# Not-left flags from one comparison on VectorE; jump codes scanned four steps after their flags

## The reference, cut to what matters

```
D = pairwise_euclidean(small=layernorm(x), large=ctx)           # 56 x 1500 for each batch
R[i, j] = D[i, j] + min(R[i-1, j], R[i, j-1], R[i-1, j-1])      # cumulative cost
# backtrack from (T1-1, T2-1):
choice = argmin([diag R[i-1, j-1], up R[i-1, j], left R[i, j-1]])
ni = i - 1 if choice <= 1 else i ;  nj = j - 1 if choice in (0, 2) else j
out[j] += rows of the other sequence met on the path
```

## Time and profile before

| what | before |
|---|---|
| median of 3 runs | 534.71 us |
| profiled execution, span from first to last instruction | 538.0 us |
| mean granted TensorE clock | 0.950 of full |
| PE busy | 431.0 us, 80% |
| DVE busy | 376.2 us, 70% |
| ACT busy | 263.5 us, 49% |
| POOL busy | 86.3 us, 16% |

### The profile page before, as it was taken

How to read it: one execution, slowest core, us unless ns; L and a number is a source line. 1 busy time by engine, 2 the same in 40 slices (tenths; PEclk the granted TensorE clock), 3 DMA queues, 4 the chain that set the end, 5 groups by cost and what they waited for, 6 DMA issues and landing times.

```text
span 538.0 us, 10079 instructions
## 1 busy us (share of the span) xinstructions
PE 431.0 (80%) x3977; PEld 249.1 (46%) x3977; DVE 376.2 (70%) x979; ACT 263.5 (49%) x452; POOL 86.3 (16%) x101
## 2 busy tenths in 40 slices
PE   3998877766788878400787899999899899989997
PEld 1344433334556665100233456566566566644444
DVE  7456999999566695885685988889788784271112
ACT  4264888765422393100102456566566567634443
POOL 2000000000100003677891000210210210200000
PEclk9999999989999999755788999999999999999999
DMA  8500266422641202882270003474383382000000
GB/s 287 214 2 0 94 201 186 130 86 86 196 115 57 59 2 66 214 192 85 60 155 18 1 1 76 100 174 94 81 174 78 98 256 60 3 0 1 0 0 17
DMA packets 28718, 50.05 MB, mean 93 GB/s; under 512 B 2464, under 2 KB 18400, under 8 KB 28672
## 3 DMA queue, kind: packets, MB, share of 16 engines
q1 hardware_dynamic: 26848, 45.74, 31.4%
q0 software_dynamic: 1536, 3.67, 2.7%
q10 hardware_dynamic: 288, 0.00, 0.0%
HBM read 39.96 MB, written 9.45 MB: 92 GB/s over the span
## 4 chain that ended last, share of the span: by engine, by line
PE 43%; DVE 37%; issue 8%; POOL 6%; ACT 3%; DMA 2%; DVEq 0%; POOLq 0%
PE banks L1586 7%; PE banks L1562 7%; POOL arena L544 6%; PE banks L1617 5%; DVE arena L1206 5%; DVE mx L1009 4%; DVE work L1235 4%; PE banks L1664 4%; PE banks L1678 4%; DVE arena L1259 2%; PE banks L1292 2%; DVE mx L1017 2%; PE banks L1430 2%; PE banks L1296 2%; DVE work L1201 2%
## 5 line engine op out<-in xcount | busy, mean ns | idle before, releaser
L1009 DVE TENSOR_REDUCE mx<-banks 112x1 f32<-112x500 f32 x168 | 106.9, 675 | 20.2 <-PE banks L1562 20.2
L771 ACT ACTIVATE arena<-banks 128x896 f32<-128x896 f32 x96 | 87.9, 917 | 51.9 <-PE banks L1617 51.2
L1314 PE MATMUL banks<-steps,one 128*128 128x500 f16 (+1 forms) x201 | 56.5, 377 | 32.3 <-DVE hcol L957 32.3
L1586 PE MATMUL banks<-arena 128*32 128x112 f32 (+1 forms) x1536 | 57.3, 265 | 2.9 <-issue 2.0
L1562 PE MATMUL banks<-ctxT,arena 128*112 128x500 bf16 x144 | 54.6, 393 | 5.6 <-issue 1.6
L1586 PEld LDWEIGHTS banks<-arena 128*32 128x32 f32 (+1 forms) x1536 | 33.7, 109 | 24.9 <-issue 20.3
L1235 DVE SCALAR_TENSOR_TENSOR work<-twice,banks,arena 128x202 f32<-128x202 f32 x68 | 29.5, 434 | 19.3 <-PE banks L1430 19.3
L1314 PEld LDWEIGHTS banks<-steps,one 128*128 128x128 f16 x201 | 20.4, 103 | 47.2 <-issue 36.7
L1617 PEld LDWEIGHTS banks<-arena,ctxT 128*128 128x128 bf16 (+1 forms) x576 | 37.3, 104 | 10.5 <-issue 2.8
L1617 PE MATMUL banks<-arena,ctxT 128*128 128x112 bf16 (+1 forms) x576 | 41.1, 213 | 0.6 <-issue 0.6
L544 POOL DMA_INDIRECT arena<-in_w_tab,idx x32 | 33.6, 1051 | 11.6 <-issue 9.4
(11 more groups left out here) (262 smaller groups left out, 751.6 us busy)
## 6 DMA issues: line engine op xcount, KB each, us to landing
ctxT<-key_parts SPq DMA_DIRECT2D x36, 375.0 KB, 6.4
key_parts<-arena SPq DMA_DIRECT2D x32, 281.2 KB, 2.8
ctxT<-in_ctx_T SPq DMA_DIRECT2D x12, 500.0 KB, 8.9
arena<-key_parts SPq DMA_DIRECT2D x12, 375.0 KB, 7.3
ctxT<-in_ctx_nat SPq DMA_DIRECT2D x5, 750.0 KB
arena<-in_ctx_nat SPq DMA_DIRECT2D x3, 750.0 KB
arena<-in_L_ffn_W SPq DMA_DIRECT2D x1, 2048.0 KB, 8.7
arena<-in_fold_w SPq DMA_DIRECT2D x1, 768.0 KB, 5.8
```

Of the source, the lines that this page charges most:

```text
L771: nc.scalar.activation(Pt[0:rows, g % 2, :].rearrange("p (a n) -> p a n", a=2), banks[0:rows, 2 + 2 * (g % 2):4 + 2 * (g % 2), 0:HQ // 2], ...
L1009: nc.vector.tensor_reduce(mx3[:, b % 2, u // NPIECE, u % NPIECE:u % NPIECE + 1], ps[k % 2][0:2 * NJ, 0:PIECE], AX_X, ALU.max).then_inc(s_m ...
L1314: nc.tensor.matmul(bank[:, 0:cols], one16[:, :], steps16[:, 0:cols], start=True, stop=True, skip_group_check=True)
L1586: last = nc.tensor.matmul(ps[6 + b % 2][q:q + 32, o:o + 2 * NJ], vals[0:rows, v0:v0 + 32], Pt[0:rows, g % 2, 2 * t * NJ:2 * (t + 1) * NJ], ...
```

## The change

The flag never is made in one DVE comparison, and ACT's sign instruction, the arrays `rise` and `rises` and two semaphores go. The scan of block k's codes moves from t = 5(k+2)+4 to t = 5(k+2), to where `rows_not_left(k)` was. The lists of the last blocks are reordered.

```diff
             def jump_inputs(k):
                 nc.vector.tensor_tensor(three(left_of(k)), R_slot(t, n, 1, C), R_slot(t, n, 0, C), ALU.is_lt)
-                nc.vector.tensor_tensor(three(rise[k % 2][:, 0:n * C]), R_slot(t + 1, n, 0, C),
-                                        three(mring[...]), ALU.subtract).then_inc(s_rise, 1)
-            def rows_not_left(k):
-                n = CODES[k][1]
-                ve.wait_ge(s_sgn, k + 1)
-                nc.vector.tensor_tensor(never[k % 2][:, 0:n * C], rises_of(k), left_of(k), ALU.is_lt
-                                        ).then_inc(s_nv, 1)
+                nc.vector.tensor_tensor(three(never_of(k)), R_slot(t + 1, n, 0, C),
+                                        three(mring[...]), ALU.is_lt).then_inc(s_nv, 1)
...
                 if t % TB == 0 and t >= 2 * TB:
-                    rows_not_left(t // TB - 2)
+                    jump_targets(t // TB - 2)
                 if t % TB == 1 and t >= TB:
                     jump_inputs(t // TB - 1)
                 if t == STEPS - 2:
-                    rows_not_left(NTB - 2)
                     ve.wait_ge(s_scan, t + 1)
-                    ve.wait_ge(s_code, NTB - 2)
                     jump_inputs(NTB - 1)
-                if t % TB == 4 and t >= 2 * TB:
-                    jump_targets(t // TB - 2)
             ve.wait_ge(s_scan, STEPS)
-            rows_not_left(NTB - 1)
             jump_inputs(NTB)
-            jump_targets(NTB - 2)
-            rows_not_left(NTB)
-            jump_targets(NTB - 1)
-            jump_targets(NTB)
+            for k in range(NTB - 2, NCODES):
+                jump_targets(k)
```

On ACT the function `rise_signs` and its calls go:

```diff
             lane_distances(2)
-            rise_signs(0)
             act.wait_ge(s_w, 16)
             key_step(0)
             lane_distances(3)
             for k in range(2, NTB):
                 for i in KEY_STEPS[k]:
                     key_step(i)
-                    if i == KEY_STEPS[k][0]:
-                        rise_signs(k - 1)
                 if k + 2 < NTB:
                     lane_distances(k + 2)
```

On PE, `jump_codes(k - 2)` keeps its place in the loop; the codes of the last two full blocks move ahead of value projections:

```diff
                 if k >= NTB - 2:
+                    if k == NTB - 1:
+                        jump_codes(NTB - 2)
                     pe.wait_ge(s_dtc, k + 1)
                     for i in range(4 * (k + 2 - NTB), 4 * (k + 3 - NTB)):
                         value(i)
-            jump_codes(NTB - 2)
+            jump_codes(NTB - 1)
             pe.wait_ge(s_kx[2], NKP - 3)
             for i in range(8, 12):
                 value(i)
-            jump_codes(NTB - 1)
```

More of the change, by code:

```diff
@@ L141, in build_gated_layers @@
         dts = work[:, 2 * N_B:4 * N_B]
-        rise = [work[:, (4 + a) * N_B:(5 + a) * N_B] for a in range(2)]
         left = [work[:, 6 * N_B + a * N_B // 2:6 * N_B + (a + 1) * N_B // 2].bitcast(F16) for a in range(2)]
-        rises = work[:, 7 * N_B:7 * N_B + N_B // 2].bitcast(F16)
         o_nv = 8 * N_B + KQW
@@ L225, in build_gated_layers @@
         left_last = sb("left_last", [P, C], F16)
+        never_last = sb("never_last", [P, C], F16)
         SUM_BANK = (6, 7, 5, 4)
@@ L323, in build_gated_layers @@
         s_scan = sem("column_scanned")
-        s_rise = sem("rises_ready")
-        s_sgn = sem("signs_of_rises_ready")
         s_nv = sem("rows_not_left_ready")
@@ L411, in piece, with never_of @@
             return a.rearrange("p (b i) -> p b i", b=NB)[:, 2 * g:2 * g + 2, n * PIECE:(n + 1) * PIECE]
-        def rises_of(k):
-            o = N_B - C if k == NCODES - 1 else 0
-            return rises[:, o:o + CODES[k][1] * C]
+        def never_of(k):
+            return never_last[:, :] if k == NCODES - 1 else never[k % 2][:, 0:CODES[k][1] * C]
         def left_of(k):
@@ L441, in _ @@
                     sp.dma_start(nat[b], ctx_nat[:, b, :, :].rearrange("c s d -> c (s d)")).then_inc(s_nat2[b], 16)
-            sp.wait_ge(s_rise, NCODES)
+            sp.wait_ge(s_nv, NCODES)
             sp.dma_start(foldw, fold_w[:, :]).then_inc(s_wqT, 16)
@@ L639, in key_step @@
                                              bias=cols[:, 1:2]).then_inc(s_kx[x], 1)
[L641 to L645, removed]
             for u in range(UN):
@@ L660, in _ @@
                     key_step(i)
-                    if i == KEY_STEPS[k][0]:
-                        rise_signs(k - 1)
                 if k + 2 < NTB:
                     lane_distances(k + 2)
-            rise_signs(NTB - 1)
-            rise_signs(NTB)
             for n in range(NKP, NKP + 2):
@@ L1175, in jump_inputs @@
                 nc.vector.tensor_tensor(three(left_of(k)), R_slot(t, n, 1, C), R_slot(t, n, 0, C), ALU.is_lt)
-                nc.vector.tensor_tensor(three(rise[k % 2][:, 0:n * C]), R_slot(t + 1, n, 0, C),
-                                        three(mring[:, t % (2 * TB) * C:(t % (2 * TB) + n) * C]), ALU.subtract
-                                        ).then_inc(s_rise, 1)
-            def rows_not_left(k):
-                n = CODES[k][1]
-                ve.wait_ge(s_sgn, k + 1)
-                nc.vector.tensor_tensor(never[k % 2][:, 0:n * C], rises_of(k), left_of(k), ALU.is_lt
+                nc.vector.tensor_tensor(three(never_of(k)), R_slot(t + 1, n, 0, C),
+                                        three(mring[:, t % (2 * TB) * C:(t % (2 * TB) + n) * C]), ALU.is_lt
                                         ).then_inc(s_nv, 1)
@@ L1373, in jump_codes @@
                                  skip_group_check=True)
-                nc.tensor.matmul(inner, never16[:, :], never[k % 2][:, 0:n * C], start=False, stop=True,
+                nc.tensor.matmul(inner, never16[:, :], never_of(k), start=False, stop=True,
                                  skip_group_check=True).then_inc(s_code, 1)
```

## The result

The changed kernel takes 560.88 us (median of 4 runs, 558.81 to 563.1) against 535.05 us for the kernel before (533.78 to 537.66): a ratio of 1.0479, 95% interval 1.0441 to 1.0517. It is slower by 25.8 us. The profiled span is 561.0 us against 538.0; that execution took 562.77 us in all, 1.8 more than its span.

What follows compares the result with a forecast made beforehand. The prediction took DVE's unbroken work in the wavefront to bound the kernel. Its terms, 3.2 + 16.7 - 0.7 + 3.9 = +23.1 us, took the median from 534.7 to 557.8 us, range 551 to 563.

Steps and rivals of the forecast that it cites:

- What bounds: Wavefront, about 53 to 134 us: DVE runs one instruction behind the other and never waits; block period 6.35 us.
- Part 1: Each block: sign, difference and L1184 go, saving 0.17 us on DVE; the new comparison saves 0.02 us.
- Part 2: Blocks 3 to 12: the moved code scan stalls 1.86 us for PE's codes; +1.67 us a block, +16.7 in all.
- The first block: Steps 10 to 14: the code scan waits for codes that follow the next distance copy; +3.2 us.
- Part 3: Last block and tail: codes are ready at step 65 and nothing is late; 9.88 against 10.61 us, -0.7.
- Part 4: Lengthened blocks: PE idles longer, so five of ten run at its lower clock, 0.78 us each; +3.9 us.
- Rival 1: Code scan's new place: the codes are ready there and the wait costs nothing; 531.9 us, chance 0.05.
- Rival 2: Blocks with two key steps (9 to 12) find their codes ready, the others wait; 546.5 us, chance 0.05.
- The step from the span to the median: Whole kernel: the runs' median lies 3.3 us below the profiled span, so 561.1 becomes 557.8 us.

Runs made afterwards that it cites:

- the run with twelve matmuls: The changed kernel with twelve matmuls, results unused, added in PE's idle time at the end of blocks 2 to 11; 558.81 us.

## Why the prediction was right

The forecast was 557.8 us, the measured median is 560.88, inside the range; the direction and the mechanism were right, and four terms were too small. The stretch grew by 26.6 us; the sum had 23.1.

- What bounds: right. Each DVE position in the block was priced by the distance between step starts, and the price held: without L1184 the block takes 6.17 to 6.18 in every run where DVE does not wait, 0.18 less than 6.35.
- Part 1, the comparison 0.02 cheaper: wrong by that much. L1161 lasts 0.67, as L1176 did; float16 output from float32 input is no faster here. The trace agrees with what the Trainium skill (VectorE: DVE Perf Modes, What auto-detection actually checks) has, no double rate with a 32-bit operand among them.
- Part 2, the wait: right in place, cause and number (eleven waits at the first step of a block, and the small one of the tail). A stall of 1.86 was forecast, 1.84 measured; the block 8.02 against 8.12. The 0.10 is 2.64 and not 2.58 to the code scan (the copy starts 0.06 behind the step), 1.12 and not 1.10 for a scan that had waited, 0.01 for the comparison and 0.01 for the three steps. Ten blocks: 1.0 us.
- The first block: +3.2 forecast, +4.5 measured (11.32 against 6.81). The next copy came 3.27 us after the first and not 2.02. About 1.0 of this is the clock, which was at 1.2 GHz there (the window 52 to 54): at full clock, in the run with twelve matmuls, the distance is 2.28 and the block 10.33. The other 0.26 is the step of the working that took all of the sign instruction's 0.51 us off this distance; only 0.25 came off (2.53 in the kernel before, from 52.83 to 55.36), and the next copy still waited 0.99 us for PE's distance columns in that run.
- Part 3, the tail: -0.7 forecast, -0.25 measured. Where the last codes come in time it takes 9.85 to 9.87, as forecast (9.88); in the changed kernel PE had waited 4.96 us for the flags, was at half clock after it, and the value projections (2.03 for twelve) made the last codes late by 0.38. The text had found nothing late there; the clock was left out of that step.
- Part 4, the clock: the price of a block was right, 0.79 against 0.78, and the count near, six blocks against five: 4.7 against 3.9. The five was a choice between none and ten, so that it came near is luck. "Some blocks low and some not" was not what happened in this profile: all ten were low for a part, four of them where it cost nothing.

The terms come to 1.0 + 1.3 + 0.45 + 0.8 = 3.5, which is the 3.5 between 23.1 and 26.6. Rival 1 (no wait) fell by the profile and became true when the codes were moved ahead of the keys: it hung on PE's list, not on DVE's. Rival 2 (the gate holds in part) fell: blocks with two key steps wait as long as those with three. That the sum gave 561.1 and the span is 561.0 is a coincidence, since the parts outside the stretch were 3.6 us shorter. The step from the span to the median was off as well: it was taken as 3.3 us, as before the change, and the median of 560.88 lies only 0.1 below the span.

## What to carry to other kernels

Before an instruction is moved ahead in its engine's list, follow its operand back through the lists of the other engines to the last semaphore that counts the consumer's own progress: here the flags were four steps early, and the codes made from them still came 2.6 us after the step they were wanted at, because of an unrelated key step ahead of them. When such a wait shows, the cure may be one line on the producer's engine, and lengthening the loop doesn't help, since the gate moves with it (the blocks grew from 6.35 to 8.12 us and still waited 1.84). And a stall can cost more than its length: PE idles in it, and its lower clock lengthened the very chain that was waited for by 0.79 us in six of ten blocks.

## What the runs showed of the hardware

The clock of PE did not follow the idle time just ahead of a burst: in the changed kernel, after 2.76 us of idleness, it fell only when PE had worked for some 1.5 us (from 81.23 to about 82.7) and the codes were done; after the next 1.91 us of idleness it was down within 0.3 us (PE starts at 89.35, and the window 90 to 92 is at half). So every block of that profile had a stretch at half clock, and blocks of 8.12 and 8.91 us took turns for most of the stretch according to where it fell. In the second profile of the same kernel some blocks had none. What decides it these runs don't say beyond this: with 12 and 19 more matmuls in the idle time no block of the ten was low. A code scan of 505 entries that had waited for PE lasted 1.20 or 1.21 us and one that had not mostly 1.18. Outside the stretch, executions of the same instructions differ by 2 to 4 us (the part ahead of the stretch took 49.2 to 52.8 us, the part from the memory layer's last update of x to the attention's first 184 to 188), which hides a gain of 1 to 2 us in the total; a block without a wait, read from one timeline, took 6.16 to 6.19 us in every run with the new comparison.
